# Second cross-attention of a two-layer perceiver block: Gram products first and without their lower left block, rows normalised later in the step

## Chip, cores and metric

The kernel runs on one core of a Trainium2 chip as one program. The metric is the device time of one execution in microseconds, the median of three runs. An execution that was profiled is looked at below in its trace; its own time is given beside the median.

## What is computed

x is 64 batches of 64 tokens with 256 features; ctx_1024 has 256 context rows for each batch. Six residual steps follow one another, each on layer-normalised x: a cross-attention with heads, a polynomial self-attention, a mixture of 16 experts (4 chosen for each token) with a shared expert, the second cross-attention, a softmax self-attention, and a quantised feed-forward with a depthwise convolution. The change is in the fourth, with an edge in the third. Cut to that:

```python
def _L1_xattn_ref(qm, km, vm):
    scale = 1.0 / jnp.sqrt(jnp.asarray(qm.shape[-1], dtype=qm.dtype))
    qkm = jnp.einsum('bqd,bkd->bqk', qm, km) * scale
    out = jnp.einsum('bqk,bkd->bqd', qkm, vm)
    return jax.nn.softmax(out, axis=-1)
...
x = x + _L0_ffn_ref(_layernorm(x, axis=-1), ...)       # routed experts: weighted sum of 4 rows a token
x = x + _L1_xattn_ref(_layernorm(x, axis=-1), ctx_1024, ctx_1024)
```

Keys and values are the same context C, and there is no softmax between the two products, so (x Cᵀ) C = x (Cᵀ C). Cᵀ C is a symmetric 256 x 256 matrix for each batch, the Gram matrix.

## The kernel before

x lies in SBUF for the whole program as 32 tiles of 128 rows (two batches each) by 256 columns. Each residual step is a block: the five engines run their own instruction streams, meet at its end, GpSimd clears the block's semaphores, and the next one begins. The blocks around the change are `experts` and `cross_attention_1`.

`experts` works through 144 slots of 128 rows: GpSimd gathers the rows (L1884), TensorE, ScalarE and VectorE compute, ScalarE writes a slot's result to one of four buffers `y` (L1944) and GpSimd scatters it to HBM (L1889). At its end GpSimd waits until all scatters have landed (L1892 and L1893).

`cross_attention_1` first has to finish the experts' sum: for each tile it adds four rows a token, gathered as `expert_y`, to x with their weights, and normalises the result. `tile_steps` (L107) writes each engine's stream: 8 steps written out, a loop over 24 tiles with four steps in its body, and 5 more written out. Every engine has its own lag, and in step s it handles different tiles:

- SyncE: context rows (L2113) and expert rows (L2115) of tile s, one after the other, each 0.52 MB (128 partitions x 1024 float32), four buffers each.
- VectorE: rows of tile s−3 normalised (L151, `xn`), row maximum of tile s−5's product (L2205), four dependent additions for tile s−2 (L2211), copy of tile s−3's transposed rows to SBUF (L2217, `xT`), statistics of tile s−2 (L135, L137), reciprocal (L2224) and last addition to x (L2226) of tile s−5.
- GpSimd: inverse standard deviation of tile s−2 (L141, L144), between VectorE's L137 and L151.
- TensorE: two transposes of tile s−3's normalised rows (L2140), then its Gram products (L2148), then tile s−4's product with its Gram matrix (L2160).
- ScalarE: exponential and its sum for tile s−5 (L2182), then tile s−3's two Gram matrices from PSUM to SBUF, scaled (L2189).

A float32 product is recorded as two passes, each with a weight load of its own (PEld). The Gram products of a batch are four: two blocks of 128 output rows, each 256 columns wide, each summed over two halves of the context. A tile has two batches, so eight products or 16 passes. The rows of the tile's own product use half of the array's columns each (64 rows a batch), so that two run side by side.

In steps 3 to 7 ScalarE also prepares feed-forward weights (`feed.absolute_sum` at L2016, `feed.taps` at L2024), which its queue loads at the block's start (L1999 to L2002, 2.1 MB). At the end, the first tiles of the next block are prepared by `following`.

## Times and profile before

| | |
|---|---|
| median of 3 runs | 2374.3 us (2369.7 to 2375.06) |
| the profiled execution | 2372.7 us, span 2370.9 us |
| TensorE busy | 2135.0 us (90%) |
| TensorE weight loads | 1592.6 us (67%) |
| VectorE busy | 1485.9 us (63%) |
| ScalarE busy | 1102.3 us (46%) |
| GpSimd busy | 984.6 us (42%) |
| second cross-attention | from 1572.0 to 1760.2 us of the span |

Times in the trace are microseconds from the span's start. PE is TensorE (matmuls), PEld its weight loads, DVE VectorE, ACT ScalarE, POOL GpSimd, SP SyncE; a q behind a name is the engine's queue of instructions or DMA commands. Matmul records overlap, since they are pipelined: the distance from start to start tells what one costs, not its recorded length. PEclk is the granted TensorE clock as a share of 2.4 GHz; 0.50 is 1.2 GHz.

### The profile page before, as it was taken

The numbers are of one execution on the slowest core, as the hardware profiler recorded it, in microseconds if no ns is written. First come the engines' busy times: TensorE is split into PE (matmuls) and PEld (weight loads), VectorE is DVE, ScalarE is ACT, GpSimd is POOL, SyncE is SP. The second block draws the span as 40 slices with busy tenths as digits, with TensorE's granted clock in tenths as the row PEclk, the third lists the DMA queues.
The fourth block names the chain that finished last, engine by engine and source line by source line (L and its number), as shares of the span: only waits on it lengthen the run. The fifth ranks groups of instructions, "written<-read, shape, count | busy, mean of one in ns | idle before, by whom it ended". The sixth has DMA issues, their size and how long they took to land. (4 is left out here: it accounts for less than half of the span.)

```text
span 2370.9 us, 57565 instructions
## 1 busy us (share of the span) xinstructions
PE 2135.0 (90%) x19526; PEld 1592.6 (67%) x19527; DVE 1485.9 (63%) x4177; ACT 1102.3 (46%) x2381; POOL 984.6 (42%) x1105
## 2 busy tenths in 40 slices
PE   6999999999999998998999999959978889777873
PEld 5888888888789986565666666636667878533332
DVE  5777777777656654883333333337767776787772
ACT  4666666666644532284222222223335555434542
POOL 4444444444300003353666666631114343136455
PEclk9999999999989978999999999979999999889996
DMA  4111111001000003041222222345520000000002
GB/s 136 32 31 30 30 34 36 30 30 40 10 11 9 9 10 109 0 195 30 82 86 88 86 86 87 86 166 195 198 91 9 9 7 9 3 1 1 0 0 71
DMA packets 120510, 128.80 MB, mean 54 GB/s; under 512 B 77537, under 2 KB 95074, under 8 KB 119138
## 3 DMA queue, kind: packets, MB, share of 16 engines
q1 hardware_dynamic: 104994, 87.12, 12.0%
q0 software_dynamic: 13824, 37.77, 5.1%
q10 hardware_dynamic: 1600, 2.72, 0.3%
q8 instruction: 54, 0.88, 0.2%
q14 instruction: 38, 0.31, 0.0%
HBM read 96.11 MB, written 27.26 MB: 52 GB/s over the span
## 5 line engine op out<-in xcount | busy, mean ns | idle before, releaser
L542 ACT ACTIVATE xa_prob<-xa_neg_s,xa_neg_max 128x256 f32<-128x256 f32 x512 | 224.5, 499 | 141.6 <-DVE xa_neg_max L420 141.6
L1907 PE MATMUL ex_ps_h<-moew_w,ex_xT 128*128 x576 | 273.1, 597 | 1.6 <-DVE ex_xT L1955 1.6
L1955 DVE COPY ex_xT<-ex_ps_x 128x256 f32<-128x256 f32 x144 | 61.2, 425 | 247.0 <-PE ex_ps_x L1914 247.0
L420 DVE CUSTOM_DVE_ANT_0 xa_neg_s<-xa_ps_s,xa_mask 128x256 f32<-128x256 f32 x512 | 191.4, 421 | 33.8 <-PE xa_ps_s L607 19.6
L1884 POOL DMA_INDIRECT ex_xg<-xn_rows,moe_in_row x144 | 139.6, 970 | 105.4 <-PE ex_ps_x L1914 96.5
L636 PEld LDWEIGHTS xa_ps_o<-xa_v,xa_probT 128*64 128x64 f32 x4096 | 141.3, 138 | 48.2 <-issue 43.0
L549 ACT ACTIVATE xa_probT<-xa_ps_s 128x512 f32<-128x512 f32 x256 | 152.0, 594 | 43.4 <-PE xa_ps_s L618 42.3
L636 PE MATMUL xa_ps_o<-xa_v,xa_probT 128*64 128x34 f32 x4096 | 170.2, 228 | 0.1
L1889 POOL DMA_INDIRECT expert_outs<-ex_y,moe_out_row x144 | 142.1, 987 | 60.9 <-ACT ex_y L1944 59.1
L618 PE MATMUL xa_ps_s<-g_ident,xa_prob 128*128 128x128 f32 x1024 | 163.9, 283 | 2.7 <-ACT xa_prob L542 2.4
L1940 ACT ACTIVATE ex_act_g<-ex_ps_h 128x256 f32<-128x256 f32 x144 | 55.2, 383 | 234.6 <-PE ex_ps_h L1907 234.6
L1921 PE MATMUL ex_ps_y<-moew_xw,ex_gT 128*128 x576 | 148.4, 380 | 1.2 <-DVE ex_gT L1965 1.2
L1907 PEld LDWEIGHTS ex_ps_h<-moew_w,ex_xT 128*128 128x128 f32 x576 | 98.7, 191 | 72.0 <-issue 72.0
L2466 PE MATMUL ff_ps_y<-ffw_h,ffw_tap 128*128 128x512 f32 x256 | 131.8, 641 | 8.1 <-DVE ff_y L2347 7.6
L2305 POOL TENSOR_TENSOR ff_y<-ff_y,ff_scale_b 128x512 f32<-128x512 f32 x64 | 82.4, 1288 | 100.2 <-ACT ff_scale_b L2401 100.2
L618 PEld LDWEIGHTS xa_ps_s<-g_ident,xa_prob 128*128 128x128 f32 x1024 | 112.7, 142 | 10.7 <-ACT xa_prob L542 3.4
L1133 POOL TENSOR_TENSOR sa_shifted<-sa_masked,sa_top 128x512 f32<-128x512 f32 x64 | 68.1, 1064 | 124.2 <-DVE sa_top L1153 124.2
L2148 PE MATMUL xb_ps_g<-xb_ctx_rows 128*128 128x256 f32 x512 | 117.8, 384 | 0.0
L367 POOL TENSOR_TENSOR xa_qz<-xa_q,xa_in_pair 128x256 fp32r<-128x256 f32 x128 | 74.5, 613 | 87.1 <-DVE xa_q L468 87.1
L1921 PEld LDWEIGHTS ex_ps_y<-moew_xw,ex_gT 128*128 128x128 f32 x576 | 98.3, 190 | 9.5 <-issue 2.1
L2148 PEld LDWEIGHTS xb_ps_g<-xb_ctx_rows 128*128 128x128 f32 x512 | 96.0, 193 | 12.2
L1944 ACT ACTIVATE ex_y<-ex_ps_y 128x256 f32<-128x256 f32 x144 | 55.2, 383 | 102.7 <-PE ex_ps_y L1921 102.7
(315 smaller groups left out, 5023.7 us busy)
## 6 DMA issues: line engine op xcount, KB each, us to landing
xa_ctxT<-in_ctxT_dram SPq DMA_DIRECT2D x32, 512.0 KB, 3.7
xb_ctx_rows<-in_ctx_rows_dram SPq DMA_DIRECT2D x32, 512.0 KB, 3.7
xb_expert_y<-expert_outs SPq DMA_DIRECT2D x32, 512.0 KB, 4.4
moew_w<-in_moe_w_dram SPq DMA_DIRECT2D x8, 1024.0 KB, 11.8
xn_rows<-rs_xn SPq DMA_DIRECT2D x8, 512.0 KB, 2.9
moew_xw<-in_moe_w_dram SPq DMA_DIRECT2D x8, 512.0 KB, 20.6
out_dram<-g_x SPq DMA_DIRECT2D x1, 4096.0 KB, 13.5
g_x<-in_x_dram SPq DMA_DIRECT2D x2, 1536.0 KB, 16.2
```

The source lines that it names most:

```text
L420: ins = nc.vector.tensor_tensor_reduce(neg_s[:, u % 2, g, :], ps_s[j][:, g * S:(g + 1) * S], mask[:, b, :], -1.0, 3e38, ALU.add, ALU.min, ...
L542: ins = nc.scalar.activation(prob[:, u % 2, i, :], neg_s[:, u % 2, i, :], ACT.Exp, bias=neg_max[:, u % 2, i:i + 1], scale=-1.0)
L549: nc.scalar.activation(probT[:, u % 2, :, :, :].rearrange("p i c t -> p (i c t)"), ps_s[u % 4][:, :], ACT.Copy).then_inc(t_ready, 1)
L618: mm = nc.tensor.transpose(ps_s[u % 4][:, k:k + P], prob[:, u % 2, g, ch * P:(ch + 1) * P], c.ident[:, :])
L636: mm = nc.tensor.matmul(ps_o[b][rows, q * 2 * D1:(q + 1) * 2 * D1], probT[:, u % 2, g, ch, rows], v[:, ap, 2 * b + ch, 2 * q:2 * q + 2, :] ...
L1884: nc.gpsimd.indirect_dma_start(xg[:, s % 4, :], None, rows, bass.IndirectOffsetOnAxis(ap=c.in_row[:, s:s + 1], axis=0)).then_inc(x_loaded[ ...
L1889: nc.gpsimd.indirect_dma_start(c.y_dram[:, :], bass.IndirectOffsetOnAxis(ap=c.out_row[:, e:e + 1], axis=0), y[:, e % 4, :], None).then_inc ...
L1907: mm = nc.tensor.matmul(ps_h[1 - par][:, :], xT[:, 1 - par, k, :], c.w1[:, own, k, :], start=(k == 0), stop=(k == KC - 1))
L1921: mm = nc.tensor.matmul(ps_y[1 - par][:, 0:E], gT[:, 1 - par, k, :], c.w2[:, own, k, :], start=(k == 0), stop=(k == KC - 1))
L2148: mm = nc.tensor.matmul(ps_g[tp][b][:, g * E:(g + 1) * E], ctx_rows[:, tq, 2 * b + k, g * P:(g + 1) * P], ctx_rows[:, tq, 2 * b + k, :], s ...
L2305: nc.gpsimd.tensor_tensor(y[:, gp, j, :], y[:, gp, j, :], scale_b[:, gp, :], ALU.mult)\
L2466: mm = nc.tensor.matmul(ps_y[j % 2][:, :], tap[:, i, j, :], h[:, j % 4, :, 2 * i:2 * i + T], start=(i == 0), stop=(i == 1))
```

## The change

Five things are done at once.

1. **Order on TensorE.** In step s the Gram products are now those of tile s, not s−3, so they stand ahead of everything that needs x. Then come two mirror transposes for tile s−2, the product of tile s−4, and last the transposes of tile s−3's normalised rows.
2. **Three blocks of four.** The lower left 128 x 128 block of the symmetric Gram matrix isn't computed. The second row block streams 128 columns instead of 256. The missing block is the transpose of the upper right one: two TensorE transposes a tile (L2162 of the new file), and a ScalarE copy (L2222).
3. **ScalarE and VectorE.** The copy of `xT` goes from VectorE to ScalarE (L2228). ScalarE takes the Gram matrix out in four pieces (256 and 128 columns for each batch), with the exponential between the two batches. `gram` has four buffers instead of two.
4. **Order on VectorE.** The first addition and the row maximum stand ahead of the normalising; the reciprocal stands between the third and the fourth addition, and the last addition to x ahead of the statistics.
5. **The start.** The wait for the experts' scatters goes from the end of `experts` to SyncE's stream in the next block. Ahead of it SyncE asks for four tiles of context. After that, each step asks for expert rows of tile s and, when the Gram products of tile s are done, context rows of tile s+4. The buffers `y` and their semaphores live on into the next block.

TensorE, in the steps written out, one step of each kernel. In the names, `xb_ps_g` is the Gram matrix in PSUM, `xb_ps_x` the transposes, `xb_ps_o` the product, `g_ident` the identity. Before:

```order
L2140 MATMUL xb_ps_x<-g_ident,xb_xn 128x128 x2
L2148 MATMUL xb_ps_g<-xb_ctx_rows 128x256 x8
L2160 MATMUL xb_ps_o<-xb_gram,xb_xT 64x256 x4
L2140 MATMUL xb_ps_x<-g_ident,xb_xn 128x128 x2
L2148 MATMUL xb_ps_g<-xb_ctx_rows 128x256 x8
```

After:

```order
L2153 MATMUL xb_ps_g<-xb_ctx_rows 128x256 x2
L2153 MATMUL xb_ps_g<-xb_ctx_rows 128x128 x2
L2153 MATMUL xb_ps_g<-xb_ctx_rows 128x256 x2
L2153 MATMUL xb_ps_g<-xb_ctx_rows 128x128 x2
L2162 MATMUL xb_ps_x<-g_ident,xb_gram 128x128 x2
L2173 MATMUL xb_ps_o<-xb_gram,xb_xT 64x256 x4
L2182 MATMUL xb_ps_x<-g_ident,xb_xn 128x128 x2
```

The transposes of x moved from the step's head to its end, half of the Gram products became narrow, and the mirror transposes are new.

VectorE, one step of those written out. `xb_neg_max` is the row maximum, `xb_rz` the reciprocal of the exponentials' sum. Before:

```order
L151 TENSOR_SCALAR xb_xn<-g_x,xb_ln_mv,xb_ln_rstd 128x256
L2205 TENSOR_REDUCE xb_neg_max<-xb_ps_o 128x1
L2211 SCALAR_TENSOR_TENSOR g_x<-xb_expert_y,moe_weight,g_x 128x256 x4
L2217 COPY xb_xT<-xb_ps_x 128x256
L135 BN_STATS xb_ln_stats<-g_x 128x6
L137 BN_AGGR xb_ln_mv<-xb_ln_stats 128x2
L2224 RECIPROCAL xb_rz<-xb_total 128x1
L2226 SCALAR_TENSOR_TENSOR g_x<-xb_ex,xb_rz,g_x 128x256
```

After:

```order
L2243 SCALAR_TENSOR_TENSOR g_x<-xb_expert_y,moe_weight,g_x 128x256
L2251 TENSOR_REDUCE xb_neg_max<-xb_ps_o 128x1
L151 TENSOR_SCALAR xb_xn<-g_x,xb_ln_mv,xb_ln_rstd 128x256
L2243 SCALAR_TENSOR_TENSOR g_x<-xb_expert_y,moe_weight,g_x 128x256 x2
L2260 RECIPROCAL xb_rz<-xb_total 128x1
L2243 SCALAR_TENSOR_TENSOR g_x<-xb_expert_y,moe_weight,g_x 128x256
L2265 SCALAR_TENSOR_TENSOR g_x<-xb_ex,xb_rz,g_x 128x256
L135 BN_STATS xb_ln_stats<-g_x 128x6
L137 BN_AGGR xb_ln_mv<-xb_ln_stats 128x2
```

The copy is gone; one addition and the maximum now stand between L137 of one step and L151 of the next.

On SyncE the first expert rows stood behind one context block and now stand behind four; those of tile s+1 stand behind a wait for tile s's Gram products.

The core of the diff:

```diff
@@ experts, gpsimd
                         y[:, e % 4, :], None).then_inc(stored[e % 4], 16)
-            for q in range(4):
-                pool.wait_ge(stored[q], 16 * (NS // 4))
...
-        gram = ph.sb("gram", [P, 2, 2, KC, E])
+        gram = ph.sb("gram", [P, 4, 2, KC, E])
@@ cross_attention_1, sync
+            for s in range(4):
+                sp.dma_start(ctx_rows[:, s, :, :], d["ctx_rows"][s, :, :, :]).then_inc(ctx_loaded[s], 16)
+            for q in range(4):
+                sp.wait_ge(c.y_stored[q], 16 * (NS // 4))
+
             def step(s, q):
                 if live(s):
-                    wait(sp, gram_done, 2 * (s - 3))
-                    sp.dma_start(ctx_rows[:, q, :, :], d["ctx_rows"][s, :, :, :]).then_inc(ctx_loaded[q], 16)
                     wait(sp, added, TOP * (s - 3))
                     sp.dma_start(expert_y[:, q, :, :], picked[s, :, :, :]).then_inc(gathered[q], 16)
-            tile_steps(sp, step, lag=0, turn=4, peel=8)
+                if live(s + 4):
+                    wait(sp, gram_done, 2 * (s + 1))
+                    sp.dma_start(ctx_rows[:, q, :, :], d["ctx_rows"][s + 4, :, :, :]).then_inc(ctx_loaded[q], 16)
+            for s in range(4):
+                step(s, s)
+            with sp.Fori(0, (NT - 8) // 4) as i:
+                for u in range(4):
+                    step(i * 4 + (4 + u), u)
+            for s in range(NT - 4, NT):
+                step(s, s % 4)
@@ cross_attention_1, tensor
                 t, o = s - 3, s - 4
-                tp, tq, op = 1 - q % 2, (q + 1) % 4, q % 2
-                if live(t):
-                    pe.wait_ge(ln.xn_ready, t + 1)
-                    wait(pe, xT_ready, t - 1)
-                    for k in range(KC):
-                        mm = nc.tensor.transpose(ps_x[tp][:, k * P:(k + 1) * P],
-                                                 ln.xn[:, tp, k * P:(k + 1) * P], c.ident[:, :])
-                    mm.then_inc(xT_done, 1)
-                    pe.wait_ge(ctx_loaded[tq], (t - tq) * 4 + 16)
+                sp_, tp, op, oq = q % 2, 1 - q % 2, q % 2, q
+                if live(s):
+                    pe.wait_ge(ctx_loaded[q], (s - q) * 4 + 16)
                     for b in range(2):
-                        wait(pe, gram_ready, 2 * (t - 2) + b + 1)
+                        wait(pe, gram_ready, GR * (s - 2) + GR // 2 * (b + 1))
                         for g in range(KC):
                             for k in range(2):
-                                mm = nc.tensor.matmul(ps_g[tp][b][:, g * E:(g + 1) * E],
-                                                      ctx_rows[:, tq, 2 * b + k, g * P:(g + 1) * P],
-                                                      ctx_rows[:, tq, 2 * b + k, :], start=(k == 0), stop=(k == 1))
+                                mm = nc.tensor.matmul(ps_g[sp_][b][:, g * (E + P):(g + 1) * E],
+                                                      ctx_rows[:, q, 2 * b + k, g * P:(g + 1) * P],
+                                                      ctx_rows[:, q, 2 * b + k, g * P:E], start=(k == 0), stop=(k == 1))
                         mm.then_inc(gram_done, 1)
+                h = s - 2
+                if live(h):
+                    pe.wait_ge(gram_ready, GR * h + GR)
+                    wait(pe, xT_ready, h - 1)
+                    for b in range(2):
+                        mm = nc.tensor.transpose(ps_x[sp_][:, E + b * P:E + (b + 1) * P],
+                                                 gram[:, (q - 2) % 4, b, 0, P:E], c.ident[:, :])
+                    mm.then_inc(mirror_done, 1)
                 if live(o):
-                    pe.wait_ge(gram_ready, 2 * o + 2)
+                    pe.wait_ge(mirror_ready, o + 1)
                     pe.wait_ge(xT_ready, o + 1)
                     wait(pe, exp_ready, o - 1)
                     if isinstance(s, int) and s == 6:
@@ -2159,8 +2172,16 @@
                         for k in range(KC):
                             mm = nc.tensor.matmul(ps_o[op][b * T:(b + 1) * T, 0:E],
                                                   xT[:, op, k, b * T:(b + 1) * T],
-                                                  gram[:, op, b, k, :], start=(k == 0), stop=(k == KC - 1))
+                                                  gram[:, oq, b, k, :], start=(k == 0), stop=(k == KC - 1))
                     mm.then_inc(o_done, 1)
+                if live(t):
+                    pe.wait_ge(ln.xn_ready, t + 1)
+                    wait(pe, xT_ready, t - 1)
+                    pe.wait_ge(mirror_ready, t + 1)
+                    for k in range(KC):
+                        mm = nc.tensor.transpose(ps_x[tp][:, k * P:(k + 1) * P],
+                                                 ln.xn[:, tp, k * P:(k + 1) * P], c.ident[:, :])
+                    mm.then_inc(xT_done, 1)
@@ cross_attention_1, scalar
+                r = s - 1
+
+                def gram_out(b):
+                    act.wait_ge(gram_done, 2 * r + b + 1)
+                    wait(act, o_done, r - 3)
+                    nc.scalar.activation(gram[:, (q - 1) % 4, b, 0, :], ps_g[par][b][:, 0:E], ACT.Copy,
+                                         scale=E ** -0.5).then_inc(gram_ready, 1)
+                    nc.scalar.activation(gram[:, (q - 1) % 4, b, 1, P:E], ps_g[par][b][:, E + P:2 * E], ACT.Copy,
+                                         scale=E ** -0.5).then_inc(gram_ready, 1)
+
+                if live(r):
+                    gram_out(0)
                 if live(o):
                     act.wait_ge(max_ready, o + 1)
                     wait(act, x_updated, o - 1)
                     nc.scalar.activation(ex[:, par, :], ps_o[par][:, 0:E], ACT.Exp,
                                          bias=neg_max[:, par:par + 1],
                                          accum_out=total[:, par:par + 1]).then_inc(exp_ready, 1)
+                if live(r):
+                    gram_out(1)
+                if live(m + 1):
+                    act.wait_ge(mirror_done, m + 2)
+                    nc.scalar.activation(gram[:, (q - 2) % 4, :, 1, 0:P],
+                                         ps_x[1 - par][:, E:2 * E].rearrange("p (b t) -> p b t", b=2), ACT.Copy)\
+                        .then_inc(mirror_ready, 1)
                 if live(m):
-                    for b in range(2):
-                        act.wait_ge(gram_done, 2 * m + b + 1)
-                        wait(act, o_done, m - 1)
-                        nc.scalar.activation(gram[:, par, b, :, :].rearrange("p k e -> p (k e)"),
-                                             ps_g[par][b][:, :], ACT.Copy, scale=E ** -0.5).then_inc(gram_ready, 1)
+                    act.wait_ge(xT_done, m + 1)
+                    wait(act, o_done, m - 1)
+                    nc.scalar.activation(xT[:, par, :, :], ps_x[par][:, 0:E].rearrange("p (k t) -> p k t", k=KC),
+                                         ACT.Copy).then_inc(xT_ready, 1)
@@ cross_attention_1, vector
-                if live(t):
-                    ln.normalise(dve, nc, t, 1 - par, xT_done)
+
+                def add(k):
+                    wait(dve, added, TOP * l + k)
+                    nc.vector.scalar_tensor_tensor(X[:, l, :], expert_y[:, (q - 2) % 4, k, :],
+                                                   c.weight[:, l, k:k + 1], X[:, l, :],
+                                                   ALU.mult, ALU.add).then_inc(added, 1)
+                if live(l):
+                    dve.wait_ge(gathered[(q - 2) % 4], (l - (q - 2) % 4) * 4 + 16)
+                    add(0)
                 if live(o):
                     dve.wait_ge(o_done, o + 1)
                     nc.vector.tensor_reduce(neg_max[:, 1 - par:2 - par], ps_o[1 - par][:, 0:E], AX.X, ALU.max,
                                             negate=True).then_inc(max_ready, 1)
+                if live(t):
+                    ln.normalise(dve, nc, t, 1 - par, xT_done)
                 if live(l):
-                    dve.wait_ge(gathered[(q - 2) % 4], (l - (q - 2) % 4) * 4 + 16)
-                    for k in range(TOP):
-                        wait(dve, added, TOP * l + k)
-                        nc.vector.scalar_tensor_tensor(X[:, l, :], expert_y[:, (q - 2) % 4, k, :],
-                                                       c.weight[:, l, k:k + 1], X[:, l, :],
-                                                       ALU.mult, ALU.add).then_inc(added, 1)
-                if live(t):
-                    dve.wait_ge(xT_done, t + 1)
-                    wait(dve, o_done, t - 1)
-                    nc.vector.tensor_copy(xT[:, 1 - par, :, :], ps_x[1 - par][:, 0:E].rearrange("p (k t) -> p k t", k=KC))\
-                        .then_inc(xT_ready, 1)
+                    add(1)
+                    add(2)
+                if live(o):
+                    dve.wait_ge(exp_ready, o + 1)
+                    nc.vector.reciprocal(rz[:, 1 - par:2 - par], total[:, 1 - par:2 - par]).then_inc(rz_ready, 1)
+                if live(l):
+                    add(3)
+                if live(o):
+                    dve.wait_ge(rz_ready, o + 1)
+                    nc.vector.scalar_tensor_tensor(X[:, o, :], ex[:, 1 - par, :], rz[:, 1 - par:2 - par], X[:, o, :],
+                                                   ALU.mult, ALU.add).then_inc(x_updated, 1)
                 if live(l):
                     wait_apart(dve, added, TOP * l + TOP, c.passed_dve)
                     ln.statistics(dve, nc, l, par)
-                if live(o):
-                    dve.wait_ge(exp_ready, o + 1)
-                    nc.vector.reciprocal(rz[:, 1 - par:2 - par], total[:, 1 - par:2 - par]).then_inc(rz_ready, 1)
-                    dve.wait_ge(rz_ready, o + 1)
-                    nc.vector.scalar_tensor_tensor(X[:, o, :], ex[:, 1 - par, :], rz[:, 1 - par:2 - par], X[:, o, :],
-                                                   ALU.mult, ALU.add).then_inc(x_updated, 1)
 
```

## Rows read from the trace of the kernel before

**Rows 1.** The page's first line: the span.

```profile
span 2370.9 us, 57565 instructions
```

**Rows 2.** Busy time by stretch; the columns are in its first line.

```profile
core 0: us, PE busy (x) PEld busy (x) DVE busy (x) ACT busy (x) POOL busy (x), PEclk, DMA share, GB/s
1565.00:1566.00 1.00, 0.00 (x0) 0.00 (x0) 0.00 (x0) 0.00 (x0) 0.00 (x0) 0.88 0.00 0
...
1587.00:1588.00 1.00, 1.00 (x3) 0.73 (x3) 0.96 (x4) 0.19 (x2) 0.00 (x0) 0.50 1.02 406
...
1589.00:1590.00 1.00, 1.00 (x5) 0.82 (x4) 0.40 (x2) 0.12 (x1) 0.57 (x1) 0.68 0.10 29
...
1651.00:1671.00 20.00, 18.45 (x100) 13.48 (x99) 15.00 (x42) 6.84 (x15) 3.71 (x8) 1.00 0.53 181
```

**Rows 3.** Timeline, block start: start, us, engine, line, out<-in, count [idle before <-releaser].

```profile
1562.43 0.96 POOL L1889 DMA_INDIRECT expert_outs<-ex_y,moe_out_row  x1 [0.98 <-ACT ex_y L1944]
1572.03 5.22 POOL L194 MEMSET sa1w_q<- 128x6144 f32 x1 [8.63 <-POOLq L76]
...
1572.41 0.42 SPq L2115 DMA_DIRECT2D xb_expert_y<-expert_outs  x1
...
1581.51 2.04 DVE L2211 SCALAR_TENSOR_TENSOR g_x<-xb_expert_y,moe_weight,g_x 128x256 f32<-128x256 f32 x4 [21.04 <-DMA xb_expert_y<-expert_outs]
...
1585.81 0.69 PE L2140 MATMUL xb_ps_x<-g_ident,xb_xn 128*128 128x128 f32 x2 [24.08 <-DVE xb_xn L151]
```

**Rows 4.** Timeline of one step in the loop, all engines.

```profile
1659.69 0.43 DVE L2205 TENSOR_REDUCE xb_neg_max<-xb_ps_o 128x1 f32<-128x256 f32 x1
...
1660.03 2.35 DVE L2211 SCALAR_TENSOR_TENSOR g_x<-xb_expert_y,moe_weight,g_x 128x256 f32 x4
...
1660.23 0.47 ACT L2182 ACTIVATE xb_ex<-xb_ps_o,xb_neg_max 128x256 f32<-128x256 f32 x1 [0.98 <-DVE xb_neg_max L2205]
...
1661.96 0.60 ACT L2189 ACTIVATE xb_gram<-xb_ps_g 128x512 f32<-128x512 f32 x1 [1.17 <-PE xb_ps_g L2148]
1662.29 0.42 DVE L2217 COPY xb_xT<-xb_ps_x 128x256 f32<-128x256 f32 x1
1662.62 0.42 DVE L135 BATCH_NORM_STATS2 xb_ln_stats<-g_x 128x6 f32 x1
1663.19 0.18 DVE L137 BATCH_NORM_AGGREGATE xb_ln_mv<-xb_ln_stats 128x2 f32<-128x6 f32 x1 [0.15 <-DVE xb_ln_stats L135]
...
1663.59 0.48 DVE L2226 SCALAR_TENSOR_TENSOR g_x<-xb_ex,xb_rz,g_x 128x256 f32 x1 [0.17 <-DVE xb_rz L2224]
...
1664.53 0.41 DVE L151 TENSOR_SCALAR xb_xn<-g_x,xb_ln_mv,xb_ln_rstd 128x256 f32 x1 [0.45 <-POOL xb_ln_rstd L144]
1664.85 0.42 DVE L2205 TENSOR_REDUCE xb_neg_max<-xb_ps_o 128x1 f32<-128x256 f32 x1
1664.99 0.20 PEld L2140 LDWEIGHTS xb_ps_x<-g_ident,xb_xn 128*128 128x128 f32 x2 [0.77 <-DVE xb_xn L151]
```

**Rows 5.** Timeline, TensorE's matmuls of one step written out ahead of the loop.

```profile
1596.47 3.62 PE L2148 MATMUL xb_ps_g<-xb_ctx_rows 128*128 128x256 f32 x16
...
1600.02 1.09 PE L2160 MATMUL xb_ps_o<-xb_gram,xb_xT 128*64 128x256 f32 x8
...
1601.14 0.44 PE L2140 MATMUL xb_ps_x<-g_ident,xb_xn 128*128 128x128 f32 x2
...
1601.41 3.62 PE L2148 MATMUL xb_ps_g<-xb_ctx_rows 128*128 128x256 f32 x16
```

**Rows 6.** Transposes of x (ns min/median/max, first and last start), and the timeline's last update.

```profile
L2140 PEld LDWEIGHTS xb_ps_x<-g_ident,xb_xn x64: 137/139/224, 1585.8 to 1749.2; 128*128 128x128 f32 x64
...
1759.67 0.48 DVE L2226 SCALAR_TENSOR_TENSOR g_x<-xb_ex,xb_rz,g_x 128x256 f32<-128x256 f32 x1
```

**Rows 7.** A product with 128 streamed columns: timeline, and its weight loads' group.

```profile
593.02 1.06 PE L696 MATMUL xa_ps_a<-xa_xT,xa_wq 128*128 128x128 f32 x8
...
L696 PEld LDWEIGHTS xa_ps_a<-xa_xT,xa_wq 128*128 128x128 f32 x256 | 32.1, 196 | 0.2
```

7 lines of the change are left out of this document (5 added, 2 removed).

## Prediction

> **What bounds the kernel now.** I read the totals first [rows 1], then the stretches around the second cross-attention [rows 2], then single instructions in three places: its start [rows 3], a step of its loop [rows 4] and a step written out before the loop [rows 5]. The span is 2370.9 us. The stage that the change touches runs from the first command of its block at 1572.03 to the last update of x at 1760.15 (1759.67 + 0.48) [rows 3, 6]: 188 us, 8% of the span. Everything else keeps its instructions and order, so the question is by how much this stage becomes shorter.
>
> In the loop, one tile costs 5.16 us from one row maximum (L2205) to the next, 1659.69 to 1664.85, and 5.27 on average: the transposes of x (L2140) start at 1585.8 for the first tile and, two a tile, at 1749.2 for the last, 163.4 / 31 [rows 4, 6]. TensorE looks like the limit, busy 18.45 of 20 us at the full clock [rows 2]. It is not quite. Its transposes at 1664.99 come after 0.77 us without weights to load, and what they waited for is VectorE's normalised rows [rows 4]. VectorE in turn stands 0.45 us before L151, for GpSimd's inverse deviation, and everything else on it in that step follows closely. So the period is VectorE's chain: 2.26 us for four additions up to the copy, 0.33 copy, 0.57 to the aggregation, 0.40 to the last addition, 0.94 to L151, 0.32 to the maximum, 0.34 to the next additions: 5.16. TensorE's own floor is read from a step where it hardly waits [rows 5]: Gram products at 1596.47, again at 1601.41, 4.94 us. Two limits 0.3 us apart: a change that lowers only one of them would bring little, and this one lowers both.
>
> **VectorE, part by part.** The copy of the transposed rows goes to ScalarE: minus 0.33. Normalising moves from the head of the step to behind one addition and the maximum. From aggregation to L151 the trace has 1.34 us (1663.19 to 1664.53), mostly GpSimd; in the new order those 1.34 us hold about 0.25 (to the first addition), 0.40 (that addition) and 0.34 (maximum) of useful work, so a wait of about 0.35 stays. The four additions depend on one another; three gaps of (2.35 − 0.48) / 3 = 0.62 and one of 0.40 make the 2.26 [rows 4]. With maximum and normalising behind the first, one gap falls from 0.62 to 0.40; the reciprocal fits in another. New step: 2.04 additions + 0.34 + 0.35 wait + 0.32 + 0.40 (last addition to x) + 0.57 + 0.25 = 4.27. The average was 0.11 above the clean step, and the loop now has more separate waits on registers: 4.4 us.
>
> **TensorE.** A tile's Gram products are eight pairs of passes over 256 columns: 3.55 us for 16 passes, 0.222 each [rows 5]. Four of the eight products now stream 128 columns. The nearest row of that shape is L696, full 128 x 128 weights against 128 float32 columns: eight passes in 1.06 us, 0.133 each [rows 7]. So 8 × (0.222 − 0.133) = 0.71 us go. Bounds: half the columns at half the price would be 0.89; if each pass had to wait for its weight load as the record gives it, 0.196 on average in L696, only 0.21. I take 0.71 since in L696 the loads are recorded as long and the passes still follow at 0.133. Added are the two mirror transposes: 0.27, as the pair at 1601.14 takes to the next product [rows 5]. Between them and the product stands one more change of operand shape; from the product to the transposes that costs up to 1.12 − 4 × 0.22 = 0.24, from Gram products to transposes nothing; I take 0.10. New floor: 4.94 − 0.71 + 0.27 + 0.10 = 4.60.
>
> A rule of the Trainium skill bears against this change ("TensorE: Matmul & The Clock Gate", Back-to-back issue gap and LDWEIGHTS): the spacing of matmuls is set by the weight load as well, and a load depends on its 128 columns and not on the moving operand, so narrowing the moving side stops paying once the load is longer. By its P / 1.2 a load is an estimated 107 ns, by which the narrow passes would save 8 × 0.115 = 0.92, about the upper bound above; the recorded 0.196 would be the case in which it binds hard.
>
> **The new period.** TensorE 4.60, VectorE 4.4: TensorE decides, and in the loop I add 0.15 for branches and register waits (VectorE's own average lies 0.11 over its clean step): 4.75. ScalarE gets more pieces: four Gram pieces, a mirror piece and a copy, none larger than the 0.60 us of a whole 512-column piece, and the exponential, 0.47 and a read of its sum [rows 4]: at most 3.6 + 0.7 = 4.3, more likely 3, since every piece has 256 columns or fewer. It is hidden: the product of tile s−4 comes in step s and wants what ScalarE copied in step s−1. The two weight sums and the taps in steps 3 to 7 use up most of that slack once. DMA: 1 MB a tile in 4.75 us is 221 GB/s, against 406 in the burst [rows 2].
>
> **The start.** The wait for the four store semaphores leaves GpSimd and goes to SyncE. It hides little. GpSimd's last scatter ends at 1563.39 and its next instruction is at 1572.03 [rows 3], but nothing moves from 1565 on [rows 2]; so of the 8.6 us at most 1.6 belong to the landing, and the rest comes behind it when the block closes. Lower bound nothing (closing waits for the same thing), upper bound 1.6; I take 1: the new block opens at 1571. Then four context blocks (2.1 MB) are asked for ahead of the first expert rows, beside 2.1 MB of feed-forward weights on ScalarE's queue. Before, the first expert rows came 9.1 us after their issue (1572.41 to 1581.51). Now they are the last of 2.1 + 2.1 + 0.5 = 4.7 MB: 11.6 us at 406 GB/s. Add 1.5 to the first byte: the 6.3 MB of the burst before take 15.5 us at that rate and end near 1589 [rows 2], so they began near 1573.5, 1.5 after the first command. That makes 1584, or some 3 us later than before. From there to the first transposes of x it was 4.3 us (1581.51 to 1585.81): 1589 instead of 1585.8. In return TensorE has done four Gram tiles by then, which it could begin at about 1576, the clock at 0.50 until it has run a while (0.50 still at 1587 and 0.68 over 1589 now [rows 2], 3.5 us after it restarts).
>
> **The sum.** From 1589.5, 28 steps with Gram products are left (tiles 4 to 31): 4 × 4.6 + 24 × 4.75 = 132.4, to 1722. Then come steps without them, at VectorE's pace: the last transposes of x lie two steps and half a one later, near 1731.2. Before, the stage ended 11 us after these (1749.2 to 1760.15); about 3 of that was the last Gram tile, which is now long done: 1739.5. That is 20.5 us earlier than 1760.2. The profiled execution took 2372.7 us, so this gives 2352.2; the median of the three runs is 2374.3, 1.6 higher. Forecast: **2353 us**, own range 2346 to 2361 (the loop's period 4.55 to 5.0, which is ±7, and the start ±3).
>
> **Rivals.**
> (a) Narrow passes cost their recorded weight load, 0.196 us. TensorE's floor is then 4.60 + 8 × 0.063 = 5.10, with the loop 5.25: 28 × 0.5 = 14 us more, 2367. For it: the records' length, and the skill's rule. Against: L696. 0.10.
> (b) A coupling makes the period about 5.0: ScalarE's queue holds the exponential behind a Gram piece and the mirror piece behind TensorE, and VectorE's reciprocal stands in front of two instructions that others want; or steps 3 to 7 fall behind by several us. Each 0.25 is 7 us: 2360. 0.20.
> (c) The earlier start counts more than I allow: the gap before the block shrinks with the wait, or the period is 4.5: 2342 to 2346. 0.10.
> (d) Slower: the first expert rows come 3 to 4 us later behind four context blocks, and the loop keeps its pace because VectorE's chain isn't shortened (GpSimd's 1.34 us simply move). Products made ahead then buy nothing: every tile still waits for its rows, and the phase ends 3.5 us later, 2378. It turns at a period of 5.3 − 3.5/28 = 5.15. Against it: copy and gap are taken away outright, 0.33 and 0.22. 0.04.
> (e) The change doesn't take effect, since the order on TensorE still makes it wait for x first. That is not so by the order: Gram products stand ahead of the transposes in each step. 0.01.
>
> **Chances.** Forecast 0.55, (a) 0.10, (b) 0.20, (c) 0.10, (d) 0.04, (e) 0.01. A measurement of this kernel tells about 0.2%, 4.7 us, from no change; no case but (d), (e) and a sum of (a) and (b) ends within it or above. Faster 0.92, same 0.05, slower 0.03. The range takes in (b) and most of (a) and (c): 2344 to 2366.
>
> **What would show it.** Right: stage length near 167 us from the block's first command; L2153 twice as many rows per tile, the narrow passes 0.13 apart; period near 4.75 with TensorE's waits at the transposes of x nearly gone; four Gram tiles before the first transposes of x, and those at 1589; the gap on GpSimd still over 6 us. Wrong in the TensorE term if narrow passes stand 0.19 apart; wrong in the VectorE term if its step is over 4.7 busy or TensorE waits again for L151 at the end of each step; wrong at the start if the first additions come before 1582 or after 1588.

## The result, and the profile after

The changed kernel takes 2340.3 us (median of 4 runs, 2338.5 to 2341.2), against 2373.7 for the kernel before (4 runs): a ratio of 0.986 [0.984, 0.988]. The direction was right and the size was not: 2353 had been predicted, with a range from 2346 beside the sum and from 2344 beside the chances.

The profiled execution took 2340.6 us, its span is 2338.8 (before 2370.9 [rows 1]).

The start of the stage, in order of time (start, length, engine, line, operation, and in brackets the idle time before it and what ended it). The first group answers to [rows 3].

```profile
1558.70 0.96 POOL L1888 DMA_INDIRECT expert_outs<-moe_y,moe_out_row  x1 [0.98 <-ACT moe_y L1941]
...
1566.58 5.22 POOL L194 MEMSET sa1w_q<- 128x6144 f32 x1 [6.92 <-POOLq L76]
...
1572.22 9.63 PE L2153 MATMUL xb_ps_g<-xb_ctx_rows 128*128 128x256 f32 x48 [14.21 <-DMA xb_ctx_rows<-in_ctx_rows_dram]
...
1581.57 2.05 DVE L2243 SCALAR_TENSOR_TENSOR g_x<-xb_expert_y,moe_weight,g_x 128x256 f32<-128x256 f32 x4 [24.83 <-DMA xb_expert_y<-expert_outs]
...
1585.95 0.44 PE L2182 MATMUL xb_ps_x<-g_ident,xb_xn 128*128 128x128 f32 x2 [1.05 <-DVE xb_xn L151]
```

The block opens at 1566.58 instead of 1572.03. Of those 5.45 us, 3.73 lie ahead of the last scatter (1562.43 before, 1558.70 now), in stages that the change doesn't touch; the gap behind it fell by 1.72. TensorE starts on the context 5.6 us after the block's first command; the first expert rows land 15.0 us after it, and the first transposes of x come 19.4 us after it.

TensorE in a step written out, answering to [rows 5]:

```profile
1586.22 2.78 PE L2153 MATMUL xb_ps_g<-xb_ctx_rows 128*128 128x256 f32 x16
1588.84 0.38 PE L2162 MATMUL xb_ps_x<-g_ident,xb_gram 128*128 128x128 f32 x2
1589.16 1.09 PE L2173 MATMUL xb_ps_o<-xb_gram,xb_xT 128*64 128x256 f32 x8
1590.18 0.44 PE L2182 MATMUL xb_ps_x<-g_ident,xb_xn 128*128 128x128 f32 x2
```

From start to start that is 2.62 for the Gram products, 0.32 the mirror pair, 1.02 the product, and the next Gram products follow at 1590.45: 4.23 us a tile. VectorE in the loop, one step and the head of the next, answering to [rows 4]:

```profile
1641.05 1.10 DVE L2243 SCALAR_TENSOR_TENSOR g_x<-xb_expert_y,moe_weight,g_x 128x256 f32 x2
1642.07 0.16 DVE L2260 RECIPROCAL xb_rz<-xb_total 128x1 f32<-128x1 f32 x1
1642.29 0.48 DVE L2243 SCALAR_TENSOR_TENSOR g_x<-xb_expert_y,moe_weight,g_x 128x256 f32 x1
1642.69 0.48 DVE L2265 SCALAR_TENSOR_TENSOR g_x<-xb_ex,xb_rz,g_x 128x256 f32 x1
1643.09 0.42 DVE L135 BATCH_NORM_STATS2 xb_ln_stats<-g_x 128x6 f32 x1
1643.66 0.18 DVE L137 BATCH_NORM_AGGREGATE xb_ln_mv<-xb_ln_stats 128x2 f32<-128x6 f32 x1 [0.15 <-DVE xb_ln_stats L135]
1643.93 0.48 DVE L2243 SCALAR_TENSOR_TENSOR g_x<-xb_expert_y,moe_weight,g_x 128x256 f32 x1
1644.33 0.42 DVE L2251 TENSOR_REDUCE xb_neg_max<-xb_ps_o 128x1 f32<-128x256 f32 x1
1645.18 0.41 DVE L151 TENSOR_SCALAR xb_xn<-g_x,xb_ln_mv,xb_ln_rstd 128x256 f32 x1 [0.43 <-POOL xb_ln_rstd L144]
```

From L151 to L151 this step takes 1645.18 − 1640.72 = 4.46 us, the one ahead of it 4.33; the wait for GpSimd before L151 is still 0.43. The transposes of x follow one another at 4.23 for the first dozen tiles, then in fours of 4.63, 4.23, 4.23, 4.37, which is 4.365. From L2182's first start at 1585.95 to its last pair, 132.9 us pass (before 163.3 [rows 6]).

Stretches (us, busy time of each engine, granted clock, share of the DMA engines, GB/s), answering to [rows 2]: the start, the loop early and late, the tail.

```profile
1572.00:1586.00 14.00, 12.73 (x69) 11.40 (x69) 3.46 (x9) 5.63 (x16) 5.31 (x10) 0.88 1.01 399
1606.00:1626.00 20.00, 20.00 (x135) 15.63 (x134) 16.62 (x47) 10.22 (x40) 3.60 (x8) 1.00 0.72 243
1646.00:1666.00 20.00, 19.78 (x130) 15.71 (x129) 16.34 (x47) 9.27 (x36) 3.65 (x9) 1.00 0.75 253
1706.00:1712.00 6.00, 2.92 (x20) 1.26 (x16) 4.91 (x14) 3.58 (x14) 1.18 (x3) 0.98 0.00 0
1712.00:1727.00 15.00, 7.90 (x30) 3.40 (x30) 11.27 (x32) 4.56 (x12) 2.66 (x6) 0.50 0.00 1
```

TensorE is full early in the loop (20.00 of 20) and has small holes later (19.78). Behind the last Gram tile, from 1712 on, the granted clock is 0.50, that is 1.2 GHz. In all, of the 32.1 us between the two profiled executions (2372.7 and 2340.6) 28.25 are the stage itself, from the block's first command to the last update of x (188.12 before, 159.87 after), 1.72 the gap, and 3.73 the stages ahead; what follows took 1.6 longer. So stage and gap give 30.0 of the 33.4 us between the medians. The other 3.4 are not shown to come from the change: they lie in stages whose instructions it leaves alone, and these differ as much between the runs below.

### The profile page after: what moved, and what is told of

Its sections match the earlier page's. It is cut to its first block and busy times, and to the rows that moved or that the text cites. A ratio compares the mean times of both kernels' runs of the same rounds, so it can differ in the third digit from the quotient of the medians.

```text
span 2338.8 us, 57804 instructions
## 1 busy us (share of the span) xinstructions
PE 2115.2 (90%) x19590; PEld 1578.8 (68%) x19591; DVE 1472.2 (63%) x4145; ACT 1112.8 (48%) x2509; POOL 980.7 (42%) x1105
## 5 line engine op out<-in xcount | busy, mean ns | idle before, releaser
L420 DVE CUSTOM_DVE_ANT_0 xa_neg_s<-xa_ps_s,xa_mask 128x256 f32<-128x256 f32 x512 | 191.4, 421 | 33.6 <-PE xa_ps_s L607 19.4
L1888 POOL DMA_INDIRECT expert_outs<-moe_y,moe_out_row x144 | 142.1, 986 | 60.9 <-ACT moe_y L1941 59.1
L2153 PE MATMUL xb_ps_g<-xb_ctx_rows 128*128 128x256 f32 (+1 forms) x512 | 90.7, 332 | 14.8 <-DMA xb_ctx_rows<-in_ctx_rows_dram 14.2
L1941 ACT ACTIVATE moe_y<-ex_ps_y 128x256 f32<-128x256 f32 x144 | 55.2, 383 | 102.7 <-PE ex_ps_y L1918 102.7
L1911 PEld LDWEIGHTS ex_ps_x<-g_ident,ex_xg 128*128 128x128 f32 x288 | 40.9, 143 | 83.0 <-issue 83.0
```

The lines of the kernel that those rows point to most:

```text
L420: ins = nc.vector.tensor_tensor_reduce(neg_s[:, u % 2, g, :], ps_s[j][:, g * S:(g + 1) * S], mask[:, b, :], -1.0, 3e38, ALU.add, ALU.min, ...
L1888: nc.gpsimd.indirect_dma_start(c.y_dram[:, :], bass.IndirectOffsetOnAxis(ap=c.out_row[:, e:e + 1], axis=0), y[:, e % 4, :], None).then_inc ...
L2153: mm = nc.tensor.matmul(ps_g[sp_][b][:, g * (E + P):(g + 1) * E], ctx_rows[:, q, 2 * b + k, g * P:(g + 1) * P], ctx_rows[:, q, 2 * b + k, ...
```

## The experiments

Each is an edit of the kernel after. "Stage" is the time from the block's first command to the last update of x, read from each trace. It is the measure here, since the total also carries what other stages do: the last scatter, ahead of which no edit changes anything, starts between 1554.8 and 1562.5 in these traces, and median less stage lies between 2178 and 2186 us. There is one trace of each run; two whose stages should be alike, stored_end and the kernel after, differ by 0.2 us in it.

### Whole Gram matrices (wide_gram)

```diff
-  ps_g[...][:, g * (E + P):(g + 1) * E],  ctx_rows[:, q, 2 * b + k, g * P:E]
+  ps_g[...][:, g * E:(g + 1) * E],        ctx_rows[:, q, 2 * b + k, :]
-  mirror transposes, their copy and their waits
```

> The changed kernel with all four blocks of the Gram matrix computed again: eight products of 256 columns a tile, no mirror transposes, the Gram matrix taken out of PSUM in four pieces of 256 columns; order and everything else as after the change. Theory 1: narrow passes cost half of wide ones (0.114 against 0.213 us) and TensorE's floor of 4.23 rests on them. Then its step is 16 x 0.213 + 0.14 to the product, 1.02 product, 0.27 transposes = 4.84 and sets the loop: 28 steps x (4.84 - 4.31) = 15 us more than the changed kernel, stage 175 us instead of 160, time 2355. Rival: the gain is from the order and VectorE alone, and the narrow blocks give nothing because a pass costs its weight load: stage 160, time 2340.

Theory 1: 2357.1 us (ratio 0.993 [0.991, 0.995]), stage 173.2. ScalarE's second piece of a Gram matrix is 256 columns wide again as well. TensorE in the loop:

```profile
1639.83 3.62 PE L2152 MATMUL xb_ps_g<-xb_ctx_rows 128*128 128x256 f32 x16
1643.38 1.09 PE L2164 MATMUL xb_ps_o<-xb_gram,xb_xT 128*64 128x256 f32 x8
1644.40 0.44 PE L2172 MATMUL xb_ps_x<-g_ident,xb_xn 128*128 128x128 f32 x2
1644.67 3.62 PE L2152 MATMUL xb_ps_g<-xb_ctx_rows 128*128 128x256 f32 x16
```

4.84 us a step, without a gap, and VectorE now waits for the product instead (0.76 us ahead of its row maximum at 1644.52). Under the new order on VectorE, the three blocks of four are worth 13.3 us of stage: 3.55 for sixteen wide passes becomes 2.62 + 0.32.

### VectorE's order of before (old_order)

```diff
-  add(0), maximum, normalise, add(1), add(2), reciprocal, add(3), last addition, statistics
+  normalise, maximum, add(0) to add(3), statistics, reciprocal, last addition
```

> The changed kernel with VectorE's old order (normalise, row maximum, four additions in a row, statistics, reciprocal, last addition), the copy of xT still on ScalarE. Theory 1: VectorE's chain sets the loop. Its old step was 5.16, less 0.33 for the copy: 4.83, on average 4.95, against 4.36 after the change: 28 x 0.6 = 17 us more, stage 177, time 2357. Rival, as I predicted: TensorE decides (4.23 to 4.36), and VectorE's order has little to do with it: stage 160 to 165, time 2340 to 2345.

2367.0 (0.998 [0.997, 1.000]), stage 182.5: longer than either theory said. The first four periods are TensorE's 4.23 (the third 4.34), and from the seventh on they come in fours that average 5.20. VectorE:

```profile
1652.60 2.34 DVE L2243 SCALAR_TENSOR_TENSOR g_x<-xb_expert_y,moe_weight,g_x 128x256 f32 x4
1655.10 0.43 DVE L135 BATCH_NORM_STATS2 xb_ln_stats<-g_x 128x6 f32 x1 [0.15 <-DVE g_x L2243]
1655.67 0.18 DVE L137 BATCH_NORM_AGGREGATE xb_ln_mv<-xb_ln_stats 128x2 f32<-128x6 f32 x1 [0.15 <-DVE xb_ln_stats L135]
1655.78 0.13 DVE L2260 RECIPROCAL xb_rz<-xb_total 128x1 f32<-128x1 f32 x1
1656.07 0.48 DVE L2262 SCALAR_TENSOR_TENSOR g_x<-xb_ex,xb_rz,g_x 128x256 f32 x1 [0.17 <-DVE xb_rz L2260]
1657.00 0.41 DVE L151 TENSOR_SCALAR xb_xn<-g_x,xb_ln_mv,xb_ln_rstd 128x256 f32 x1 [0.45 <-POOL xb_ln_rstd L144]
```

From aggregation to L151 it is 1.33 us again, as in [rows 4], with only the last addition in between, and it leads the whole step: L151 releases TensorE, which waits 0.77 at its transposes. The copy has left VectorE here too, and that shortens the loop by 0.11 only: the same fours average 5.31 before. The rows tell why. From the first addition to the statistics it was 2.59 us with the copy between (1660.03 to 1662.62 [rows 4]) and is 2.50 without it, since the statistics have to wait for the last addition anyway (the 0.15 in the row). The copy stood mostly in that wait.

### One addition fewer (three_adds)

The fourth weighted expert output isn't added to x. Nothing else changes.

> The changed kernel without the last of the four weighted additions of expert rows on VectorE (the sum over experts lacks its fourth term). Theory 1: VectorE sets the later part of the loop, 4.36 against TensorE's 4.23. With one addition less its step is about 3.8, so every loop step takes 4.23 to the end of the loop and the steps without Gram products get shorter too: stage 155 to 156, time 2336. Rival: the 0.13 over 4.23 is TensorE's own loop cost (branch, register waits), one step in four at 4.63 stays: stage 158 to 159 (the last steps alone shorter), time 2339.

2332.6 (0.984 [0.982, 0.987]), stage 152.9, and the period is 4.23 (the third 4.35) up to the last tile with Gram products. So the steps of 4.63 and 4.37 are VectorE's, and 4.23 is TensorE's floor. The 4.63 reaches TensorE by way of ScalarE: its Gram pieces stand behind the exponential, which waits for VectorE's maximum, and the next Gram products of the kernel after wait for these pieces:

```profile
1654.90 2.69 PEld L2153 LDWEIGHTS xb_ps_g<-xb_ctx_rows 128*128 128x128 f32 x16 [0.38 <-ACT xb_gram L2207]
```

The first 27 periods and the start make 2.5 of the 7 us; the others come from the tail, where two periods fall to 2.4.

### The copy back on VectorE (copy_dve)

```diff
-  nc.scalar.activation(xT[...], ps_x[...], ACT.Copy)
+  nc.vector.tensor_copy(xT[...], ps_x[...])      # last in VectorE's step
```

> The changed kernel with the copy of xT on VectorE again, as the last instruction of its step. Theory 1 (VectorE's chain sets the loop): its step grows by the copy's 0.35 to about 4.7: 28 x 0.37 = 10 us more, stage 170, time 2350. Rival (a): ScalarE's extra work was the tighter end and gets shorter here: stage 160 or less. Rival (b): the copy now waits for transposes at the end of TensorE's step, and VectorE stands: period over 5, stage over 180, time over 2360.

This theory fell. 2344.5 (0.989 [0.987, 0.991]), stage 158.95 instead of 159.87, the number of rival (a), with the period at 4.23 for 20 tiles. VectorE:

```profile
1665.62 0.18 DVE L137 BATCH_NORM_AGGREGATE xb_ln_mv<-xb_ln_stats 128x2 f32<-128x6 f32 x1 [0.15 <-DVE xb_ln_stats L135]
1665.72 0.42 DVE L2268 COPY xb_xT<-xb_ps_x 128x256 f32<-128x256 f32 x1
1666.07 0.48 DVE L2238 SCALAR_TENSOR_TENSOR g_x<-xb_expert_y,moe_weight,g_x 128x256 f32 x1
1666.46 0.42 DVE L2246 TENSOR_REDUCE xb_neg_max<-xb_ps_o 128x1 f32<-128x256 f32 x1
1667.00 0.41 DVE L151 TENSOR_SCALAR xb_xn<-g_x,xb_ln_mv,xb_ln_rstd 128x256 f32 x1
```

The step from L151 to L151 is 1667.00 − 1662.69 = 4.31, with 0.35 us more work in it, against 4.46 and 4.33. The copy stands where VectorE used to wait 0.43 for GpSimd, and 0.12 of that wait is left. So in this place the copy costs nothing: four steps from L151 to L151 average 4.34, against 4.365 in the kernel after. From aggregation to L151 it is 1.38 in three of four steps here, and 1.29 to 1.52 there; what makes GpSimd's part vary isn't shown.

From the first L151 to the last VectorE needs 1.9 us less here. About half of that is one step at the start, and there rival (a) has a point. In the kernel after, ScalarE prepares feed-forward weights and copies `xT` in the same steps, and VectorE waits for the exponential behind that work:

```profile
1595.12 0.16 DVE L2260 RECIPROCAL xb_rz<-xb_total 128x1 f32<-128x1 f32 x1 [0.96 <-ACT xb_ex L2215]
```

That step of VectorE takes 4.90 there and 3.97 here. At the end 0.9 us are lost again: the last transposes start 1.36 us after their L151, against 0.47.

### Both large parts undone (wide_old)

wide_gram and old_order together.

> The kernel after, with both large parts undone at once: whole Gram matrices on TensorE (four blocks of four, no mirror transposes) and VectorE's order of before (normalise, maximum, four additions, statistics, reciprocal, last addition); the copy stays on ScalarE, the products four tiles ahead. With one undone at a time the period was 4.84 (whole matrices) and 5.20 (old order). Theory A (the period is the longer of two chains): about 5.2, stage 183 to 185, total 2367, as with the old order alone; the narrow blocks are worth nothing under the old order. Theory B (the two add up, since each step passes from one engine to the other): period 4.23 + 0.61 + 0.97 = 5.8, stage 196 to 200, total 2380. A stage between 186 and 190 would say that running four tiles ahead brings nothing by itself against before (188.1).

2363.2 (0.997 [0.996, 0.999]), stage 183.2. Theory A: the longer of two chains counts. VectorE begins with a lead, that is, rows are normalised well before TensorE comes to transpose them; as long as it lasts, the period is TensorE's (4.84 for sixteen tiles, the third 4.96), and then VectorE's, 5.21 on average. The four stages:

| stage, us | VectorE old order | new order | order is worth |
|---|---|---|---|
| whole Gram matrices | 183.2 | 173.2 | 10.0 |
| three blocks of four | 182.5 | 159.9 | 22.6 |
| the blocks are worth | 0.7 | 13.3 | |

Each alone brings 0.7 and 10.0, both together 23.3. The 0.7 can hardly be told from nothing: the medians, 2367.0 and 2363.2, go the other way. The remaining 4.9 us to the stage before (188.1) are the products four tiles ahead, the copy's move and the other transfers at the start; no run parts these further. The traces say where they arise: the first transposes of x come 7.8 us later after the block's first command than before, the 31 periods take 9.7 less, and what follows them 3.0 less.

### The wait for the scatters (stored_end)

```diff
+            for q in range(4):
+                pool.wait_ge(stored[q], 16 * (NS // 4))
```

> The kernel after, with the wait for the four store semaphores put back at the end of the experts' instructions on GpSimd (SyncE's wait stays as well). Theory A (the wait stood in series with the closing of the block): the gap from the last scatter to the block's first command goes from 7.88 back to about 9.6 us, the stage from the block's first command stays at 159.9, total 1.7 us longer, 2342. Rival B (the wait is free, and the 1.7 us in the gap came from elsewhere): gap 7.9, total unchanged, 2340.

The gap is back at 9.59 us and the stage is 160.05; the median is 2345.8 (0.989 [0.987, 0.992]), 5.5 above the kernel after, of which only 1.7 can be the gap's.

```profile
1570.95 5.22 POOL L194 MEMSET sa1w_q<- 128x6144 f32 x1 [8.62 <-POOLq L76]
```

Theory A: the wait stood in series with the closing of the block and cost 1.71 us. The other 6.9 us of idle time on GpSimd stay without it.

### Four tries at the start

rows_second: expert rows 0 are asked for behind context block 0.

> The kernel after, with the first expert rows asked for behind the first context block instead of behind all four. Theory A (the start is set by all five transfers together: TensorE makes four Gram tiles ahead of the first transposes of x, and the fourth block now lands last): first addition at about 9 us from the block's first command instead of 15.0, but the first transposes of x only at 17.5 to 19 instead of 19.4, stage 158 to 160, total 2339 to 2341. Rival B (the expert rows alone set the start): transposes of x at 13.5, stage 154, total 2335.

weights_later: the feed-forward weights are asked for on SyncE's queue after the first expert rows and the fifth context block.

> The kernel after, with the 2.1 MB of feed-forward weights asked for on SyncE's queue behind the first expert rows, instead of on ScalarE's queue at the start of the block. Theory A (the start is bandwidth: 4.7 MB stand in front of the first expert rows, the weights are 2.1 of them): first addition at 15.0 - 5 = 9.5 to 10.5 us from the first command, first transposes of x at 14 to 15.5, stage 155 to 156, total 2336. Rival B (the two queues do not share evenly, or the fourth context block arrives late for another reason): first addition at 13 or later, stage 158 to 160, total 2339 or more.

Both missed, on the other side. The first addition came early (9.2 and 9.9 us after the block's first command), the first transposes of x late (22.6 and 20.5), stages 163.1 and 161.3; ratios 0.989 [0.987, 0.992] and 0.989 [0.986, 0.991]. VectorE in weights_later:

```profile
1582.75 0.18 DVE L137 BATCH_NORM_AGGREGATE xb_ln_mv<-xb_ln_stats 128x2 f32<-128x6 f32 x1
1589.96 0.48 DVE L2243 SCALAR_TENSOR_TENSOR g_x<-xb_expert_y,moe_weight,g_x 128x256 f32<-128x256 f32 x1 [7.03 <-DMA xb_expert_y<-expert_outs]
1590.36 0.41 DVE L151 TENSOR_SCALAR xb_xn<-g_x,xb_ln_mv,xb_ln_rstd 128x256 f32<-128x256 f32 x1
```

The new order has its price here. The first addition of tile 1 stands ahead of the normalising of tile 0, so tile 0 waits for tile 1's rows. Those are asked for on SyncE only behind a wait for the first Gram tile, and in weights_later behind the 2.1 MB of weights too. TensorE, done with its four Gram tiles, waits 2.97 us for L151 there.

In rows_second VectorE is held up in the same way, but it isn't what decides:

```profile
1575.19 7.17 PE L2155 MATMUL xb_ps_g<-xb_ctx_rows 128*128 128x256 f32 x32 [2.02 <-DMA xb_ctx_rows<-in_ctx_rows_dram]
1580.72 0.41 DVE L151 TENSOR_SCALAR xb_xn<-g_x,xb_ln_mv,xb_ln_rstd 128x256 f32<-128x256 f32 x1
1585.25 0.38 PE L2184 MATMUL xb_ps_x<-g_ident,xb_xn 128*128 128x128 f32 x2
```

Tile 0 is normalised 4.5 us before its transposes. TensorE has to finish four Gram tiles first; it waited for the second context block, and its granted clock was 0.62 over 1575 to 1579. The next expectation gives VectorE's order as the cause for both runs; that holds for weights_later alone.

woven: context 0 and 1, rows 0, context 2, rows 1, context 3, rows 2, the weights, rows 3.

> The kernel after, with another order of the first transfers on SyncE's queue: context block 0, 1, expert rows 0, context block 2, rows 1, context block 3, rows 2, then the feed-forward weights (which leave ScalarE's queue), then rows 3. In the two runs that moved one of these the transposes of x came later, not sooner, because VectorE's first addition for tile 1 stands ahead of the normalising of tile 0 and rows 1 were asked for only after the first Gram products. Theory A (that is the cause): with rows 1 early, VectorE is ready by 13 us from the block's first command, TensorE with its four Gram tiles at about 17, the first transposes of x at 17 to 17.8 instead of 19.4, stage 157.5 to 158.5. Rival B (the weights come too late for the sums in ScalarE's step 3, or the fifth context block does): stage 160 or more.

First transposes at 17.7, as theory A has it, but the stage is 161.5 (0.991 [0.988, 0.993]): rival B. TensorE and ScalarE:

```profile
1585.85 0.38 PE L2192 MATMUL xb_ps_x<-g_ident,xb_xn 128*128 128x128 f32 x2
1589.29 2.86 PE L2163 MATMUL xb_ps_g<-xb_ctx_rows 128*128 128x256 f32 x16 [3.06 <-ACT xb_gram L2215]
```

```profile
1586.70 1.91 ACT L2013 ACTIVATE ffw_tap<-ffw_w_raw 128x2048 f32<-128x2048 f32 x1 [3.11 <-DMA ffw_cb<-in_ff_cb_dram]
```

ScalarE's sum over the weights, in its step 3, now waits 3.1 us for them, and the Gram copies are queued behind it. The fifth context block, asked for behind the weights at 1577.38, takes 11.6 us to land, to 1589.0, so it would have held the next Gram products nearly as long; both halves of rival B came. What is gained at tile 0 is lost at tile 1.

woven_warm: the same, with products of no use on TensorE until the first context block is there.

> The order of transfers of the run woven, and ahead of the first Gram products twenty products of no use (identity against identity, overwritten), while TensorE waits for the first context block. The first three Gram tiles took 9.6 us in the kernel after, the first of them at the granted clock 0.50, against 2.62 a tile at the full clock. Theory A (TensorE's clock sets when the four Gram tiles are done): they take 10.5 to 11.5 us instead of 12.5 to 13.5, the first transposes of x another 1.5 to 2.5 us earlier than in woven, stage 155.5 to 156.5. Rival B (the context blocks arrive too late for that): within 0.5 of woven.

Three Gram tiles take 8.02 us instead of 9.63, and the first transposes come at 16.9. The stage is 162.1 (0.990 [0.988, 0.992]), as the weights are still awaited. The products of no use also held TensorE for 6.0 us after the first command, where woven started on its context after 3.7, and the fifth Gram tile came after a wait of 3.0 us and took 4.3 us instead of 2.7.

best: woven_warm and the copy on VectorE.

> The run woven_warm, with the copy of the transposed rows on VectorE as the last instruction of its step instead of on ScalarE. The copy there took the loop's period from 4.37 to 4.25 on average. Theory A: stage 1 us shorter than woven_warm, 154.5 to 155.5; total 2335 against 2340.3 for the kernel after, 0.985 of before. Rival B (at the start of the stage the copy on VectorE delays the first steps by what it gains later): stage equal to woven_warm's.

Stage 159.4, total 2343.0 (0.989 [0.987, 0.991]): 2.75 us of stage less than woven_warm, 1.6 of them up to the second transposes of x and 1.1 behind them, and 0.5 less than the kernel after, which no total here can tell. No edit of the start alone beat the kernel after.

### The tail (busy_tail)

Four products of no use in each of the four steps behind the last Gram tile.

> The kernel after, with four products of no use (their result is overwritten by nothing and read by nobody) behind the transposes in each of the four steps that follow the last Gram tile, so that TensorE stays occupied while the tail runs. Theory A (the tail is slow since TensorE's granted clock falls to 0.50 from 1712 on): the clock stays up, a product L2173 takes 1.09 us instead of 1.98 and a pair of transposes 0.44 instead of 0.69, three steps shorter by 0.9 to 1.2 each, stage 157 to 158.5, total 2338 to 2339. Rival B (the tail is VectorE's and GpSimd's chain, and what TensorE saves is hidden): stage within 0.5 of 159.9 or longer, total 2340 or more.

2337.9 (0.986 [0.984, 0.988]), stage 160.4: rival B. The granted clock over 1712 to 1727 is 0.92 instead of 0.50,

```profile
1712.00:1727.00 15.00, 11.53 (x60) 7.30 (x58) 9.86 (x27) 4.74 (x13) 3.67 (x8) 0.92 0.01 2
```

and the last two products take 1.09 us, but the time doesn't follow. From L151 to L151 the last two steps of VectorE are 3.95 and 3.8 us in both traces, at either clock. The products of no use also take TensorE's time: the second-last period of the transposes is 5.0 instead of 3.9. So the run shows that VectorE paces the tail, and not exactly what the clock alone costs. VectorE has two instructions of the next stage ahead of the last row maximum:

```profile
1721.11 0.73 DVE L233 TENSOR_SCALAR sa1w_xn<-g_x,sa1w_ln_mv,sa1w_ln_rstd 128x256 f32<-128x256 f32 x2
1721.76 1.75 DVE L211 TENSOR_TENSOR sa1w_wqkv<-sa1w_wqkv 128x1536 fp32r<-128x1536 f32 x1
1723.43 0.42 DVE L2256 TENSOR_REDUCE xb_neg_max<-xb_ps_o 128x1 f32<-128x256 f32 x1
```

## Why the prediction was off, step by step

The sum foresaw 2352.2 us for a profiled execution; it took 2340.6. Of the 11.6, 3.7 are the earlier stages' and no step of the prediction, 0.7 the gap (1.72 against the 1 taken, over the upper bound of 1.6), and −1.6 what follows the stage. The stage has the rest, 8.6 with the roundings: 159.9 against 1739.5 − 1571 = 168.5. That the profiled execution came 11.6 early and not 8 is in part luck, the 3.7.

- **The start: +1.4.** First transposes of x 19.4 us after the first command instead of 18; first additions at 15.0 instead of 13. In the trace's own time they came at 1581.6, ahead of the 1582 that was named as a sign of error, only because the block opened 4.4 us earlier than forecast. The transfers ran at 399 GB/s and in the order foreseen, a little later.
- **TensorE's floor: the step that failed.** 4.60 was taken and 4.23 came, in the steps written out and in the loop. The narrow pass: 1.06 / 8 from L696 [rows 7] divides a recorded length that holds the last pass's own 0.28 once. From start to start it is (1.06 − 0.28) / 7 = 0.111. A wide pass is (3.62 − 0.38) / 15 = 0.216 by [rows 5]; eight of each take 2.62 now, 1.73 + 0.89, which gives 0.111 for the narrow one again. Gram products were 16 × 0.222 in the prediction, minus 0.71: 2.84. Measured 2.62, a miss of 0.22. The further change of operand shape, 0.10, costs 0.05 (the mirror pair 0.32 against 0.27). From the product to the transposes it was 1.12 in [rows 5] and is 1.02: another 0.10 that had been read as fixed, and it was a wait. In the trace of before VectorE's normalising starts 0.47 ahead of those transposes, the distance at which they start whenever they waited for it (1718.37 and 1718.84 in the trace after), so the 4.94 held 0.10 of VectorE's chain:

```profile
1600.67 0.41 DVE L151 TENSOR_SCALAR xb_xn<-g_x,xb_ln_mv,xb_ln_rstd 128x256 f32<-128x256 f32 x1 [0.45 <-POOL xb_ln_rstd L144]
```

Together 0.37.

The recorded lengths of single passes, 0.28 over 128 columns and 0.38 over 256, stand in the groups of L2153 by shape (busy, mean ns of one | idle; the wide mean holds the slow ones of the start):

```profile
L2153 PE MATMUL xb_ps_g<-xb_ctx_rows 128*128 128x256 f32 x256 | 67.5, 387 | 14.8 <-DMA xb_ctx_rows<-in_ctx_rows_dram 14.2
L2153 PE MATMUL xb_ps_g<-xb_ctx_rows 128*128 128x128 f32 x256 | 39.3, 277 | 0.0
```

- **The 0.15 for the loop: also wrong.** TensorE's steps in the loop are 4.23 as well. The allowance came from VectorE's average and was put on TensorE.
- **Which engine decides.** The forecast said TensorE at 4.75 over VectorE at 4.4. VectorE's 4.4 was nearly right (4.365, with 0.43 of wait left in every second step against the 0.35 expected), and with the real floor of 4.23 it is VectorE that decides late in the loop: three_adds shows it. Over 27 periods from the first transposes the average is 4.31, since the lead that VectorE has at the start is used up only after a dozen tiles (from L151 to its transposes 1.37 us for the sixth tile, 0.47 for the thirteenth); the prediction has 4.73. That is 11.3 us, the larger part of the miss.
- **The tail: +2.0 in the last four periods, −0.7 after the last transposes.** The prediction's 9.2 us for "two steps and half a one" would be 11.0 at its own 4.4; 11.9 passed. The clock's fall was not in the prediction. By busy_tail it isn't what paces VectorE's steps there, though the last transposes take 0.69 instead of 0.44 us by it; the two instructions of the next stage ahead of the last maximum stood there before the change too.
- **The copy: a part put at 0.33 that was worth 0.11** in its old place (old_order) and costs nothing at the end of the step (copy_dve). VectorE's chain was rightly found, through L137, GpSimd and L151, but the copy was priced at the distance from its start to the next instruction's, and that next instruction, the statistics, had to wait for the last addition in any case. The part that pays is what stands between L137 and L151 (old_order).
- **The rivals.** (a), the recorded weight load as the price of a pass, is refuted by 0.111 where the record has 0.196 [rows 7]. Of the Trainium skill's rule ("TensorE: Matmul & The Clock Gate", Back-to-back issue gap and LDWEIGHTS) the trace agrees in size and doesn't prove it: the estimate was 107 ns, the passes stand 0.111 apart. But 0.111 is also about half of the 0.216 of a pass over 256 columns, so the moving columns alone account for it, and no run here narrows these passes further, which could part the two. (b), a coupling to 5.0, didn't come; its way through ScalarE exists, but costs 0.38 a time (four times between 1600 and 1700) and 0.96 once at the start. Nor did (d). (c) was the right direction and had 0.10; its second half, a shorter period, is what happened, at 4.31 and not 4.5, and its 2342 to 2346 was still too slow. That two chains bound the loop and that lowering one alone brings little is shown by the table under wide_old.
- **Slips.** 1760.2 − 1739.5 is 20.7, not 20.5, and two ranges are given, from 2346 and from 2344. Neither matters for the miss.

The lesson of the range is that its low end took the period's error as 0.2 us, while TensorE's floor alone was off by 0.37 in one direction.

## What to carry to other kernels

Read what a matmul costs from start to start; where a group's recorded length is all there is, take the last matmul's own length away before dividing by one less than their number. When two engines bound a loop within some per cent, make a table of either change alone and both: here 0.7 and 10.0 us alone were 23.3 together. And ask of an engine with waits in its step whether work taken off it lies on the chain at all, or in the wait of the next instruction for an earlier one; putting independent work between the two ends of a round trip through another engine is what paid here.
